# Attention maxima transposed on VectorE, contexts read by ScalarE, and the first batch finished at the end of each attention layer

## The reference

```python
x = x + tanh(g_xattn[0]) * deformable_attention(ctx, layernorm(x), ...)
x = x + tanh(g_ffn[0])   * int8_matmul(layernorm(x), ...)
x = x + tanh(g_xattn[1]) * attention(layernorm(x), ctx, ...)   # 16 heads of 8
x = x + tanh(g_ffn[1])   * mixture_of_8_experts(layernorm(x), ...)
x = x + tanh(g_xattn[2]) * attention(layernorm(x), ctx, ...)   # 16 heads of 16
x = x + tanh(g_ffn[2])   * ternary_glu(layernorm(x), ...)
x = x + tanh(g_xattn[3]) * attention(layernorm(x), ctx, ...)   # 8 heads of 4
x = x + tanh(g_ffn[3])   * rwkv_channel_mix(layernorm(x), ...)

# each of the three attentions, per head:
A = softmax(scale * einsum('bqd,bkd->bqk', q, k), axis=-1)     # 512 queries, 1024 keys
o = einsum('bqk,bkd->bqd', A, v)                               # then all heads @ Wo
```

## Time and profile before

| | before |
|---|---|
| median of 3 runs | 1188.35 us (1186.31 to 1188.7) |
| profiled execution | 1189.92 us, span 1187.9 us |
| TensorE busy | 1054.0 us (89%) |
| VectorE busy | 783.8 us (66%) |
| ScalarE busy | 492.1 us (41%) |
| GpSimd busy | 206.3 us (17%) |
| attention, first to last exponential | layer 1 209.2 to 403.2, layer 2 599.3 to 798.6, layer 3 1043.4 to 1143.3 |

### The profile page before, as it was taken

One profiled execution on the slowest core, in us unless ns is written; L12 is line 12 of the kernel. 1 busy time (PEld: TensorE's weight loads), 2 busy tenths in 40 slices (PEclk: granted clock), 3 DMA queues, 4 the chain that ended last, 5 costly groups with the idle time before them and its releaser, 6 DMA issues.

```text
span 1187.9 us, 17076 instructions
## 1 busy us (share of the span) xinstructions
PE 1054.0 (89%) x6429; PEld 601.9 (51%) x6429; DVE 783.8 (66%) x1448; ACT 492.1 (41%) x722; POOL 206.3 (17%) x251
## 2 busy tenths in 40 slices
PE   8788958999989878996899998997989997999998
PEld 4233433444434448993344444444778785344445
DVE  5979778888788232555588886824545555688616
ACT  2642430667667501110157674772212211067452
POOL 4556410111110020004111111101300402011000
PEclk9989976899999958998779999999989999689799
DMA  6779701013310516961512231101443440100001
GB/s 209 242 250 332 250 26 61 21 40 121 110 39 12 160 49 227 361 240 51 173 37 47 61 100 29 35 2 36 134 150 106 129 141 2 31 11 12 1 28 35
DMA packets 79571, 121.79 MB, mean 103 GB/s; under 512 B 10125, under 2 KB 53296, under 8 KB 79482
## 3 DMA queue, kind: packets, MB, share of 16 engines
q1 hardware_dynamic: 59782, 79.41, 21.8%
q10 hardware_dynamic: 18932, 39.10, 9.3%
q0 software_dynamic: 768, 2.10, 0.6%
HBM read 92.45 MB, written 27.81 MB: 101 GB/s over the span
## 4 chain that ended last, share of the span: by engine, by line
PE 60%; DVE 26%; DMA 4%; issue 4%; ACT 3%; POOL 2%; ACTq 0%; SPq 0%; DVEq 0%; POOLq 0%
DVE arena L2116 13%; PE bank L1451 11%; PE bank L1411 11%; PE bank L1635 11%; PE st_bank L1563 3%; PE bank L1575 3%; PE st_bank L1436 3%; DMA kparts<-arena 2%; PE bank L1218 2%; PE st_bank L1635 2%; PE st_bank L1368 2%; DVE xn L1746 2%; PE bank L1481 2%; PE bank L1417 1%; DVE bnst L1726 1%
## 5 line engine op out<-in xcount | busy, mean ns | idle before, releaser
L2116 DVE TENSOR_REDUCE arena<-bank 128x1 f32<-128x512 f32 x640 | 400.2, 683 | 66.4 <-PE bank L1411 66.3
L1098 ACT ACTIVATE arena<-st_bank 128x1024 f32<-128x1024 f32 x320 | 316.1, 1022 | 159.9 <-PE st_bank L1436 158.5
L1411 PE MATMUL bank<-g_a 64*128 64x512 f32 x480 | 185.2, 519 | 12.3 <-DVE arena L2116 2.9
L1451 PE MATMUL bank<-arena,vaug 128*9 128x256 f32 (+2 forms) x2560 | 175.1, 392 | 1.7 <-ACT arena L1098 1.7
L1411 PEld LDWEIGHTS bank<-g_a 64*128 64x128 f32 x480 | 75.9, 200 | 122.1 <-DVE arena L2116 83.6
L1635 PE MATMUL bank<-g_a,g_w 128*128 128x512 f32 x512 | 120.3, 396 | 4.3 <-DVE g_w L2320 3.2
L1436 PE MATMUL st_bank<-g_a 64*128 64x512 f32 x480 | 116.9, 443 | 0.0
L1635 PEld LDWEIGHTS bank<-g_a,g_w 128*128 128x128 f32 x512 | 97.7, 192 | 26.1 <-DVE g_w L2320 3.6
L1451 PEld LDWEIGHTS bank<-arena,vaug 128*9 128x9 f32 (+2 forms) x2560 | 56.6, 93 | 80.5 <-issue 42.7
L1411 PE MATMUL bank<-g_x,g_a 64*128 64x512 f32 x160 | 64.2, 531 | 9.5 <-DVE arena L2116 4.3
L1436 PEld LDWEIGHTS st_bank<-g_a 64*128 64x128 f32 x480 | 61.3, 191 | 6.6 <-issue 0.5
(11 more groups left out here) (301 smaller groups left out, 1400.3 us busy)
## 6 DMA issues: line engine op xcount, KB each, us to landing
arena<-in_glu_w SPq DMA_DIRECT2D x39, 512.0 KB, 3.4
arena<-kv_table SPq DMA_DIRECT2D x11, 1024.0 KB, 8.1
ctxT<-in_glu_w ACTq DMA_DIRECT2D x22, 512.0 KB, 6.6
arena<-in_w SPq DMA_DIRECT2D x20, 512.0 KB, 6.0
kparts<-arena ACTq DMA_DIRECT2D x12, 512.0 KB, 5.6
arena<-in_w ACTq DMA_DIRECT2D x12, 512.0 KB, 3.5
xnT<-kv_table SPq DMA_DIRECT2D x5, 1024.0 KB, 7.6
g_a<-kparts SPq DMA_DIRECT2D x24, 192.0 KB
```

Source lines behind the costliest of these rows:

```text
L1098: act.activation(prob[sl % PROBS], st_bank[sl % 2][:], ACT.Exp, scale=scale).then_inc(exp_ready, 1)
L1411: pe.matmul(bank[TURN_BANKS[place % 3]], Qc[gi % KQ_BUFS][rows, hh, qt * P:(qt + 1) * P], Kc[gi % KQ_BUFS][rows, half * CH:(half + 1) * CH ...
L1451: ins = pe.matmul(bank[7][at:at + dh + 1, 0:D], vaug[l][:, b * KT + 2 * m + i, h0 + hh, :], tiles[:, a], start=(m == 0 and i == 0), stop=( ...
L2116: dve.tensor_reduce(mxh[gi % 2][:, col, hf:hf + 1], bank[TURN_BANKS[place % 3]], AX.X, ALU.max).then_inc(max_red, 1)
```

## The change

The turn of the maxima leaves TensorE and ScalarE. A new step `shift` comes directly behind a group's last maximum: VectorE transposes a 128x32 tile (8 columns of maxima and 24 zeros) in blocks of 32x32, and GpSimd makes the two parts from it, now on 128x32. K has rows of -1 in place of 1, so nothing is negated. Both heads' queries lie in one 128x512 tile, where each head had a 512-column half of its own, so a transfer can write one row of each head. The transposed maxima lie in four blocks of 32 partitions, and SyncE issues one DMA for each block and part: eight of 2x4x32, in place of four of 1x4x128. `LEAD` becomes `HALVES` + 8 = 24.

The contexts, except a layer's last, are copied from the bank by ScalarE (after it has waited for TensorE's turn of them), and GpSimd takes the power -1 of the sums and multiplies. The step `normal` stands directly behind `context`. GpSimd clears shift rows in slot 1 of a group.

The finish of batch 0 begins in slot `NGROUPS[l] * KT - LEAD // HG + 1` of the layer, 11 slots before its end, one step in every slot; VectorE copies out its `heads`. Those slots have no `hold`.

```diff
+SQ = 32
+SHIFT_DMAS = P // SQ * SHIFT_ROWS
...
-LEAD = HALVES + 14
+LEAD = HALVES + 8
...
-        first = (b + 1) * batch * KT + CTX_SLOT + 3
+        first = NGROUPS[l] * KT - LEAD // HG + 1
...
-            finish[first + FINISH_EVERY * i] = step
+            finish[first + i] = step
...
-            if u > HALVES and u % HALVES == TURN_LAG:
-                turn("turn", u // HALVES - 1)
-            if u == total:
-                turn("turn", NGROUPS[l] - 1)
+            if u % HALVES == 0:
+                steps.append(("shift", u // HALVES - 1))
...
     def context(g):
         turn("context", g)
-        later.append((u + NORMAL_AFTER, ("normal", *steps[-1][1:])))
+        steps.append(("normal", *steps[-1][1:]))
...
-            if u == total and LEAD + HG * (sl - 1) >= total:
+            if u == total and LEAD + HG * (sl - 1) >= total and sl not in finish:
                 for _ in range(TAIL_HOLDS):
                     turn("hold")
...
             def shift_load(l, g):
                 gi = GROUP0[l] + g
                 sp.wait_ge(max_lo, gi + 1)
-                for h in range(HG):
+                for r in range(P // SQ):
                     for i in range(SHIFT_ROWS):
-                        row = h * HALF_P + i
-                        sp.dma_start(Qc[gi % KQ_BUFS][row:row + 1, h].bitcast(F32).rearrange("o (q n) -> o q n", n=P),
-                                     shp[gi % 2][i][h * QT:(h + 1) * QT, :].bitcast(F32)).then_inc(shift_ld[gi % KQ_BUFS], 16)
+                        sp.dma_start(Qc[gi % KQ_BUFS][i:i + HALF_P + 1:HALF_P].bitcast(F32).rearrange("h (q r n) -> h q r n", q=QT, n=SQ)[:, :, r],
+                                     shp[gi % 2][i][r * SQ:r * SQ + HG * QT].bitcast(F32)).then_inc(shift_ld[gi % KQ_BUFS], 16)
...
+                    elif step[0] == "score" and step[2] == CLEAR_SLOT and KQ_BUFS <= step[1] + 3 < NGROUPS[l]:
+                        shift_rows(l, step[1] + 3, shifts, contexts)
+                    elif step[0] == "normal" and step[1] < NGROUPS[l] - 1:
...
+                        ch.link(pool.tensor_tensor(rsum_p, sums[:, :, :, dh], bc(minus_one[:, 0:1].unsqueeze(2), [P, QT, 2 * HG]), ALU.pow))
+                        pool.tensor_tensor(dst, sums[:, :, :, 0:dh], bc(rsum_p.unsqueeze(3), [P, QT, 2 * HG, dh]), ALU.mult).then_inc(norm_ready, 1)
...
-                    elif step[0] == "turn":
+                    elif step[0] == "normal" and step[1] < NGROUPS[l] - 1:
                         _, g, place = step
...
-                        act.activation(shn[gi % 2][0:HG * QT, :], bank[TURN_BANKS[place % 3]][0:HG * QT, 0:P], ACT.Copy, scale=-1.0).then_inc(max_neg, 1)
...
+                        act.wait_ge(pv_tr, k + 1)
...
+                        act.activation(context_sums(l, k), turned[:, :, :, 0:dh + 1], ACT.Copy).then_inc(ctx_read, 1)
...
-                        pe.wait_ge(shift_ld[gi % KQ_BUFS], 16 * HG * SHIFT_ROWS * (gi // KQ_BUFS + 1))
+                        pe.wait_ge(shift_ld[gi % KQ_BUFS], 16 * SHIFT_DMAS * (gi // KQ_BUFS + 1))
...
+                def turn_max(g):
+                    gi = GROUP0[l] + g
+                    dve.wait_ge(max_fin, gi + 1)
+                    if gi >= 2:
+                        dve.wait_ge(max_lo, gi - 1)
+                    dve.transpose(mxt[gi % 2], mxg[gi % 2]).then_inc(max_tr, 1)
```

More of the change, by code:

```diff
@@ L695, in queries_load @@
                 sp.wait_ge(qp_st[k % 2], 16 * PARTS * (k // 2 + 1))
-                load_rows(l, g, [Qc[gi % KQ_BUFS][:, i] for i in range(HG)], qparts[l], slice(b * S, (b + 1) * S))
+                load_rows(l, g, Qc[gi % KQ_BUFS], qparts[l], slice(b * S, (b + 1) * S))
             def shift_load(l, g):
@@ L1110, in attention @@
                         act.activation(pvs[gi % 2], bank[7][:, 0:D], ACT.Copy).then_inc(pv_evac, 1)
-                    elif step[0] == "heads":
+                    elif step[0] == "heads" and step[1][0] == B - 1:
                         _, (b, c), place = step
@@ L1383, in attention @@
                 order = schedule(l)
-                rotation = [step for step in order if step[0] in ("max", "turn", "context", "heads", "out", "hold")]
+                rotation = [step for step in order if step[0] in ("max", "context", "heads", "out", "hold")]
                 def bank_read(place):
@@ L1397, in bank_read @@
                         return x_ready, stage * NT + what[0] * QT + what[1] * 2 + 2
-                    if kind == "turn":
-                        return max_neg, GROUP0[l] + what + 1
+                    if what < NGROUPS[l] - 1:
+                        return ctx_read, contexts_read(l, what)
                     return norm_ready, (GROUP0[l] + what) // 2 + 1
@@ L1410, in row_max @@
                         pe.wait_ge(*bank_read(place))
-                    pe.matmul(bank[TURN_BANKS[place % 3]], Qc[gi % KQ_BUFS][rows, hh, qt * P:(qt + 1) * P], Kc[gi % KQ_BUFS][rows, half * CH:(half + 1) * CH],
+                    pe.matmul(bank[TURN_BANKS[place % 3]], Qc[gi % KQ_BUFS][rows, qt * P:(qt + 1) * P], Kc[gi % KQ_BUFS][rows, half * CH:(half + 1) * CH],
                               start=True, stop=True).then_inc(max_mm, 1)
@@ L1490, in attention @@
                         row_max(*step[1:])
-                    elif step[0] == "turn":
-                        turn_max(*step[1:])
                     elif step[0] == "hold":
@@ L2105, in attention @@
                 dve.memset(bank[7], 0.0).then_inc(pv_done, 1)
+                for i in range(2):
+                    ins = dve.memset(mxg[i][:, HG * QT:], 0.0)
+                ch.link(ins)
                 if l > 1:
@@ L2140, in attention @@
                         reduce_half(*step[1:])
-                    elif step[0] == "normal":
+                    elif step[0] == "shift":
+                        turn_max(step[1])
+                    elif step[0] == "heads" and step[1][0] < B - 1:
+                        _, (b, c), place = step
+                        dve.wait_ge(ctxT_mm, CTX_BANKS0[l] + b * EC[l] + c + 1)
+                        dve.tensor_copy(xnT[0:n, c, b * CH:(b + 1) * CH], bank[TURN_BANKS[place % 3]][0:n, :]).then_inc(ctxT_ready, 1)
+                    elif step[0] == "normal" and step[1] == NGROUPS[l] - 1:
                         normalise_context(*step[1:])
```

109 lines of the change are left out of this document (55 added, 54 removed).

## The result

The changed kernel takes 1243.69 us (median of 4 runs, 1242.79 to 1254.63), the kernel before 1188.53 us in the same comparison (1186.31 to 1193.44): a ratio of 1.048, 95% interval 1.041 to 1.055. It is slower by 55 us, where 66 us were forecast. A second comparison, further down, gave 1238.10 us and 1.040 (1.035 to 1.045).

The account below looks back on a forecast made before the run. A loop through three rotating banks bounds the kernel; late shifts would then set the pace. From 1189.9 us, replacing 493.2 of attention with 37 x 14.5 + 3 x 7.3 + 0.9, less 1.6, gives 1254 us; range 1150 to 1290.

Parts of the forecast that it names:

- What bounds it now: Attention before the change: a loop through three rotating banks, TensorE and VectorE, 2.68 us per slot pair, 11.84 a group.
- The shift chain: Reduction to landed shifts: 7.0 us needed, 3.7 available, so 3.3 late in every group; loop 13.8 us, not 11.84.
- cheap-issue rival: SyncE issues shift DMAs as cheaply as key loads, 0.36 us each: group 12.0 us, total 1162 us; chance 0.25.
- The clock: Waits lower TensorE's clock, 1.5 us for a pair of slots; half taken, 0.7 us, giving 14.5 us a group.
- in every group: Rival: TensorE's clock falls in each group, 15.3 us a group, 1284 us in total; chance 0.08.
- The sum: Whole kernel: 1189.9 - 493.2 + 37 x 14.5 + 3 x 7.3 + 0.9 = 1256.0, less 1.6: 1254 us.
- The finish in the tail: Batch 0's finish in a layer's last two groups costs nothing; without the wait for the shift some 3 us a layer.
- The start of the layer: Unchanged: scores begin 7.1 us after the small reduction, and the new chain needs 7.1 too.
- Nothing late from GpSimd and ScalarE: GpSimd's power (4.2 us if it grows with columns) and product stay off the path; ScalarE copies contexts instead.
- The signs: Profile checks: eight DMAs over 4.3 us, TensorE idle some 3 us a group, over 100 in total, groups 13.8 to 15.3.
- Even and odd alike: Even and odd groups equally long, 13.8 to 15.3 us; longer even groups would mean the context step sets the pace.
- The last sign: Steady parts well under full clock would show the forecast wrong: the clock falls more than counted.

Follow-up runs that it names:

- lead 30: Changed kernel with only the lead of the maxima over the scores put back from 24 to 30 halves: 1144.62 us, ratio 0.959.
- second profile: Profile of the changed kernel run again unaltered, against the kernel before: 1238.10 us, ratio 1.040.
- the hold products: Changed kernel with five useless 64x512 products on TensorE before each group's first score, from the second group on: 1211.75 us, ratio 1.019.
- the fastest kernel: Changed kernel with four shift DMAs a group (high part of the maximum alone) and a lead of 26 halves: 1138.29 us, ratio 0.955.
- lead 28: Changed kernel with a lead of 28 halves in place of 24: 1141.94 us, ratio 0.957.
- four DMAs: Changed kernel, lead still 24 halves, with four shift DMAs a group in place of eight (high part of the maximum alone): 1149.09 us, ratio 0.965.
- lead 26: Changed kernel with a lead of 26 halves in place of 24: 1159.78 us, ratio 0.974.

## Why the prediction was right, point by point

**What bounds it now** held: the loop over the banks at its old pace shows again with lead 30, and the forecast of 11.2 us for a group without the turn measured 11.18. The 0.6 us that I gave to the turn alone are 0.48 for it and, on the mean, some 0.2 for the contexts.

**The shift chain** was the right mechanism, term by term at full clock:

| term | predicted | measured |
|---|---|---|
| first score to the end of the small reduction | 5.0 + 1.65 | 6.60 |
| to SyncE's first issue | 1.0 | 0.94 |
| first to last of eight issues | 7 x 0.62 = 4.34 | 3.78 |
| last issue to the first score | 1.7 + 0.15 | 1.55 |
| loop | 13.8 | 12.87 |

The mis-sized terms are the issue and the landing. I took 0.57 us from the earlier trace rows, and the two-row shape takes 0.495; with the step 0.54. That, and 0.3 at the landing, is nearly all of the 0.9 us a group. It is nearer to my value than to the key loads' 0.36, and above the 0.46 from which the cheap-issue rival would have won. At 0.54 us it did not, by 0.08 us a DMA. From the first to the last of eight issues it is 3.8 us, the last one's way to the score 1.55, and halving their number gave some 90 us. The rule that the time to start a DMA is usually small beside the DMA itself (the Trainium skill, DMA: Bandwidth & Descriptors, section Issuing engines are not separate DMA queues) does not hold for these.

**The clock** was under-sized in layer 1. I took 0.7 us a group, 1.5 for a fall and a fall in half the groups. The price was right: 27.3 us for two groups in layer 2 are 1.6 over two bare loops. How often it falls was a guess. By groups, the mean of all but the last two in each layer is 14.37, 13.61 and 13.58 us against 12.86, so 1.5 in layer 1 (1.0 in the second profile) and 0.7 in layers 2 and 3; the hold products, which took most falls away, gave 26 to 32 us. So the rival "in every group" had layer 1 of the first profile nearly right, and half the groups is what layers 2 and 3 show: there the fall comes in every second group. A fall in each round, as the Trainium skill describes it (TensorE: Matmul & The Clock Gate, section HAM oscillation), is thus nearly what layer 1 of the first profile shows; layers 2 and 3, and the first ten groups of layer 1 in the second profile, do not.

**The sum** is nearer than its terms, and that is luck: the loop was 34 us too long in all, the clock's part 13 and the tail's 7 too short (the two clears on VectorE take 0.16 us a layer, not 0.3). 34 steady groups at 13.92 and the last two of each layer at 70.4 us make 543.6, where I had 559.3 (37 x 14.5 + 3 x 7.3 + 0.9). With the 3 us from outside that is 1256 - 16 + 3 = 1243, the time of the profiled execution.

**The finish in the tail** does not cost nothing. The last two groups of the layers take 21.4, 25.3 and 23.7 us, where a steady one (13.92) and 7.3 would be 21.2: 7 us in all, in layers 2 and 3 alone. Without the wait, with lead 30, it costs 1.8, 7.0 and 6.6 us, where I had named some 3 a layer. TensorE is the engine there, busy without a gap from 834 to 850 us; two of the four row blocks of batch 0 on the timeline of the changed kernel in layer 2:

```profile
839.23 1.13 PE L1489 MATMUL bank<-wo,xnT 128*128 128x256 f32 x4
840.29 0.69 PE L1491 MATMUL bank<-bo,onesf 1*128 1x256 f32 x2
840.91 1.13 PE L1489 MATMUL bank<-wo,xnT 128*128 128x256 f32 x4
841.97 0.69 PE L1491 MATMUL bank<-bo,onesf 1*128 1x256 f32 x2
```

An `out` step holds TensorE for 3.4 us there, with a bias product of one row that layer 1 does not have. The old cost in the middle did go: no group between 300 and 390 us is longer than 15.1.

**The start of the layer** held within 0.7 us: 6.47 us from the end of the small reduction (209.56) to the first score (216.03), where 7.1 was forecast. **Nothing late from GpSimd and ScalarE** held too: in the kernel with holds, groups with and without a context are alike at 12.86 us in layers 2 and 3. The power of 16 columns takes 2.90 us, under the bound of 4.2 (from which I worked that out, show the power of -1/2, not of -1):

```profile
L873 POOL TENSOR_TENSOR arena<-arena,minus_one x17: 2897/2901/2909, 254.1 to 1180.9; 128x16 f32<-128x16 f32 x17
```

**The signs.** Eight DMAs take 4.28 us (over 4.3 forecast, so just short of it; under 3.3 would have refuted it). TensorE waits before the first score in 36 groups, but for 2.1 us and 76 in all, not 3 and 100: the same 0.9 us as above. "Even and odd alike" was wrong in layers 2 and 3. By my own list that was a sign that the context sets the pace, and this reading would have been wrong as well: it was the clock, as the holds show. The last sign, a steady part well under full clock, came in layer 1 alone: 0.87 (0.91 from 225 to 425 us in the second profile) beside 0.94 and 0.93, which are about what 3.4 us at 0.50 in every 27.3 us give. By these signs the mechanism was right in the chain and incomplete in the clock.

**The size of the stakes** I had seen for the number of DMAs, but not for the lead: before the change the shifts were over 3 us early by the sum, so one slot less should have cost nothing (no run tried one slot), and here the first slot is worth 84 us, the others 15 together.

## What to carry to other kernels

A run-ahead distance is a budget for one chain; add that chain up, issue of each DMA included, before the distance is cut, and leave a slot where bulk loads are issued beside it. When a chain sets the pace, the number of DMAs on one queue is a term like any other: here 0.54 us each, in every round. A wait of 2 us in a loop costs more than itself where it takes the clock with it, and a profile with two lengths of round should be read with the clock beside it before a step is blamed.

## What the runs showed of the hardware that I had not expected

- SyncE's issue of an SBUF-to-SBUF DMA goes neither by bytes nor by pieces: 0.573 us into one row, be it 4 pieces of 512 bytes (2 KB) or of 128 bytes (0.5 KB), but 0.495 us into two rows with 8 pieces of 128 bytes (1 KB). The loads of 24 rows of keys from DRAM on the same queue take 0.40 us at the median, less than either.
- A stage that the change does not touch took 8 us more in one execution than in another, with TensorE's clock lower for longer. Layer 0 on the kernel before and on the changed one, by window, with the same 35 products of TensorE in both:

```profile
60.00:80.00 20.00, 16.95 (x35) 6.15 (x36) 12.41 (x19) 8.31 (x23) 10.60 (x3) 0.81 0.91 284
```

```profile
64.00:86.00 22.00, 21.98 (x35) 7.30 (x36) 9.36 (x12) 6.91 (x19) 9.03 (x2) 0.65 0.72 234
```

In the first the clock is full again for these products from 68 us on, in the second only from 80. The first exponential of layer 1 lies between 205.7 and 216.9 us in 14 profiles, at 216.9 and 210.5 for the same program. The runs of the changed kernel span 12 and 15 us in the two comparisons, those of the fastest kernel 4; whether the waits of the changed kernel are the cause was not tested.
- The falls can lock to the loop: in layer 2 of the changed kernel they come 27.3 us apart, seven in a row, always in the same group of two, and again so in the second profile. The four that the hold products left in layer 1 have the same distance.
- An SBUF-to-SBUF DMA of 1 KB that reaches the score 1.55 us after its issue takes longer beside a 512 KB load on ScalarE's queue, and on the whole the more so the closer before it the load is issued. In waits for a shift: 3.54 to 3.75 us with the load 0.4 us before it (lead 28, layer 1), 2.8 to 3.3 with 0.5 to 0.9 (four DMAs), 2.2 to 2.7 with 1.0 to 1.6 (lead 26), 1.55 to 1.81 with 2.6 to 3.0 (the changed kernel, layer 1). A load of 4 KB 1.3 or 1.6 us before it changes nothing (1.54 and 1.53, lead 26).
